# Attention in front of a mixture of experts: the row of maxima carried by a second copy of the queries, and a batch's work in another order

## What is computed

```python
scores = jnp.einsum('bkgsd,bktd->bkgst', qh, kh) / scale     # qh: normalised x, scale = 4
weights = jax.nn.softmax(scores, axis=-1)
out = jnp.einsum('bkgst,bktd->bkgsd', weights, vh)
...
x = x + jnp.tanh(g_xattn[0]) * _L0_xattn_ref(_layernorm(x, axis=-1), ctx_512, ctx_512)
x = x + jnp.tanh(g_ffn[0]) * _L0_ffn_ref(_layernorm(x, axis=-1), ...)
```

## Time and profile before

| | us |
|---|---|
| median of 3 runs | 1440.05 |
| lowest, highest | 1434.08, 1441.21 |
| the profiled execution | 1444.12 |
| its span | 1442.2 |
| PE busy in the span | 1332.6 (92%) |
| DVE busy | 932.8 (65%) |
| ACT busy | 543.3 (38%) |
| POOL busy | 412.3 (29%) |

### The profile page before, as it was taken

How to read it: one execution, slowest core, us unless ns; L and a number is a source line. 1 busy time by engine, 2 the same in 40 slices (tenths; PEclk the granted TensorE clock), 3 DMA queues, 4 the chain that set the end, 5 groups by cost and what they waited for, 6 DMA issues and landing times.

```text
span 1442.2 us, 33176 instructions
## 1 busy us (share of the span) xinstructions
PE 1332.6 (92%) x12082; PEld 918.3 (64%) x12082; DVE 932.8 (65%) x1627; ACT 543.3 (38%) x847; POOL 412.3 (29%) x470
## 2 busy tenths in 40 slices
PE   3799989797895789989999999999999999999996
PEld 2444444444442667777777777777777777777773
DVE  4897787979765896855545555545444444446887
ACT  2666666767655432222222222222222222222220
POOL 4565455545443710011111111111111111004454
PEclk9965575859555589999999999999999999999998
DMA  6443333334332751136255363546163631167665
GB/s 241 140 133 113 110 132 131 132 104 137 110 133 99 267 190 60 59 132 205 73 179 191 124 212 102 194 144 222 60 211 124 197 108 59 44 212 234 212 206 188
DMA packets 98794, 213.50 MB, mean 148 GB/s; under 512 B 11824, under 2 KB 12336, under 8 KB 98736
## 3 DMA queue, kind: packets, MB, share of 16 engines
q1 hardware_dynamic: 87536, 176.02, 36.1%
q0 software_dynamic: 11200, 36.71, 8.1%
HBM read 228.26 MB, written 66.06 MB: 204 GB/s over the span
## 4 chain that ended last, share of the span: by engine, by line
PE 82%; DVE 8%; issue 4%; DMA 3%; ACT 2%; POOL 1%; DVEq 0%; SPq 0%; ACTq 0%; POOLq 0%
PE PS L1395 38%; PE PS L1414 19%; PE PS L1268 5%; PE PS L1240 5%; PE PS L1252 3%; PE PS L1383 3%; PE PS L1276 3%; DVE negm L841 2%; PE PS L1222 2%; PE PS L1256 1%; DVE xn L827 1%; DMA xnd<-xhl 1%; DMA negR<-negT 1%; PE PS L1286 1%; DVE st L798 1%
## 5 line engine op out<-in xcount | busy, mean ns | idle before, releaser
L1414 PE MATMUL PS<-wb,ghl 128*128 128x512 f16 x1296 | 291.5, 382 | 5.8 <-issue 3.2
L1395 PE MATMUL PS<-uhl,wb 128*128 128x256 f16 x2592 | 293.5, 273 | 2.1 <-DVE uhl L1090 2.1
L1395 PE MATMUL PS<-xT,wb 128*128 128x256 f16 x2592 | 291.8, 273 | 1.1 <-DVE xT L1080 1.1
L1395 PEld LDWEIGHTS PS<-xT,wb 128*128 128x128 f16 x2592 | 253.5, 98 | 30.6 <-issue 1.2
L1395 PEld LDWEIGHTS PS<-uhl,wb 128*128 128x128 f16 x2592 | 252.2, 98 | 31.5 <-DVE uhl L1090 2.4
L1414 PEld LDWEIGHTS PS<-wb,ghl 128*128 128x128 f16 x1296 | 127.4, 98 | 149.9 <-issue 10.2
L841 DVE TENSOR_REDUCE negm<-PS 128x8 f16<-128x1024 f32 x128 | 156.1, 1220 | 75.2 <-PE PS L1240 65.5
L604 POOL COPY ixr<-idx 128x2 int32 x38 | 7.0, 184 | 604.0 <-PE PS L1383 478.4
L1097 DVE TENSOR_TENSOR g<-sl,u 128x512 f32<-128x512 f32 x108 | 74.7, 691 | 146.9 <-ACT sl L761 146.8
L761 ACT ACTIVATE sl<-PS,bb 128x256 f32<-128x256 f32 x216 | 90.5, 470 | 209.7 <-PE PS L1395 209.7
L752 ACT ACTIVATE u<-PS,bb 128x256 f32<-128x256 f32 x216 | 90.4, 470 | 197.0 <-PE PS L1395 164.0
(11 more groups left out here) (153 smaller groups left out, 1597.3 us busy)
## 6 DMA issues: line engine op xcount, KB each, us to landing
wb<-wsc SPq DMA_DIRECT2D x126, 1024.0 KB
wst<-in_wall SPq DMA_DIRECT2D x32, 768.0 KB, 5.9
wsc<-whl SPq DMA_DIRECT2D x32, 768.0 KB, 4.2
ysl<-yb SPq DMA_DIRECT2D x46, 512.0 KB
bd<-in_bdown SPq DMA_DIRECT2D x42, 256.0 KB
X<-in_x SPq DMA_DIRECT2D x8, 1024.0 KB, 8.5
xnd<-xhl SPq DMA_DIRECT2D x32, 256.0 KB, 3.0
xs<-xnd SPq DMA_DIRECT2D x32, 256.0 KB
```

Source lines behind the costliest of these rows:

```text
L1395: ins = pe.matmul(bank[:, hf, (m % 2) * TT:(m % 2 + 1) * TT], wb[:, par, l, k, w, m * P:(m + 1) * P], rhs(x, k), start=(n == 0), stop=(n = ...
L1414: ins = pe.matmul(PS[2][:, t, :], ghl[:, x, k, t * P:(t + 1) * P], wb[:, par, 2, k, w, :], start=(n == 0), stop=(n == len(TERMS) - 1))
```

## The change

The one-row pass is dropped. `negR` becomes `qB`, of the same size: a second copy of a batch's transposed queries, made by a DMA from `qT` (`queries_again`, 256 KB). The row of maxima is then written by DMA over row 16 of each strip of `qB`, and row 16 of the second key version holds ones (a memset on POOL at the start) where it held zeros. So the second pass, now of 32 rows, multiplies the low keys by the high queries and subtracts the maxima in one product. The other 15 rows of low queries meet zeros. SP waits for the copy before it sends a batch's first row of maxima.

The lists of PE, DVE, ACT and SP are put in a new order. The core of the diff, with lines left out:

```diff
+            def queries_again(half, par, quad):
+                b = number(half, par)
+                if isinstance(b, int) and b < 2:
+                    sp.wait_ge(S["qT_ready"], b + 1)
+                else:
+                    sp.wait_ge(S["t_done"], UNITS * (b - 1))
+                sp.dma_start(qB[:, par, :, :, :], qT[:, quad, :, :, :]).then_inc(qB_in[par], 16)
             def neg_rows(half, par, pair):
+                if pair == 0:
+                    sp.wait_ge(qB_in[par], 16 * (half + 1))
+                    sp.nop(nofuse=True)
                 sp.wait_ge(S["negT_ready"], 2 * number(half, par) + pair + 1)
-                sp.dma_start(negR[0::STRIP, par, pair, :, :], negT[:, pair, :]).then_inc(neg_in[pair], 16)
+                sp.dma_start(qB[D::STRIP, par, pair, :, :], negT[:, pair, :]).then_inc(neg_in[pair], 16)
...
                 if nx is not None:
                     neg_rows(*nx[:2], 1)
+                if after is not None:
+                    queries_again(*after)
...
+            for par in range(2):
+                g.memset(kx[:, par, 1, :, 1, 0:1], 1.0).then_inc(S["vone"], 1)
...
                 exps(half, par, 1)
+                if not start:
+                    evac_o(*((half - 1, 1) if par == 0 else (half, 0)), 1)
                 if after is not None:
                     evac_q(*after)
-                if not start:
-                    evac_o(*((half - 1, 1) if par == 0 else (half, 0)), 1)
                 exps(half, par, 2)
+                evac_o(half, par, 0)
+                exps(half, par, 3)
                 weights_hi(half, par)
-                exps(half, par, 3)
-                evac_o(half, par, 0)
...
-                for w, rows in ((0, STRIP), (1, D)):
+                for w in range(2):
                     for odd in range(2):
-                        part = strip(u, odd, rows)
-                        pe.matmul(Tb[:, odd, :], kT[part, quad, w, u // 2, :], qT[part, quad, u // 2, :, :].rearrange("p m c -> p (m c)"),
-                                  start=w == 0, stop=False)
-                for odd in range(2):
-                    part = strip(u, odd, 1)
-                    ins = pe.matmul(Tb[:, odd, :], one16[part, :], negR[part, par, u // 2, :, :].rearrange("p m c -> p (m c)"),
-                                    start=False, stop=True)
+                        part = strip(u, odd, STRIP)
+                        moving = (qT[part, quad, u // 2, :, :], qB[part, par, u // 2, :, :])[w]
+                        ins = pe.matmul(Tb[:, odd, :], kT[part, quad, w, u // 2, :], moving.rearrange("p m c -> p (m c)"),
+                                        start=w == 0, stop=w == 1)
                 ins.then_inc(S["t_done"], 1)
+                if ahead is not None:
+                    scores_max(*ahead)
```

More of the change, by code:

```diff
@@ L192, in program @@
         neg_in = [sem(f"neg_in{j}") for j in range(2)]
+        qB_in = [sem(f"qB_in{j}") for j in range(2)]
         x_in = [sem(f"x_in{c}") for c in range(XC)]
@@ L324, in body @@
                 nx = follow(half, par, quad, 1)
+                after = follow(half, par, quad, 2)
                 start = isinstance(half, int) and number(half, par) == 0
@@ L893, in body @@
                 start = isinstance(half, int) and number(half, par) == 0
[L894 to L898, removed]
+                fourth = follow(half, par, quad, 4)
                 if nx is not None:
                     maxes(*nx[:2], 1)
+                if after is not None:
+                    evac_k(*after)
+                if nx is not None:
+                    maxes(*nx[:2], 2)
                 if not start:
                     normalise(*pv, 0)
-                if after is not None:
-                    evac_k(*after)
                 if isinstance(half, int) and number(half, par) + 2 < XC:
@@ L907, in body @@
                 if nx is not None:
-                    maxes(*nx[:2], 2)
-                weights64(half, par)
+                    evac_neg(*nx[:2], 0)
+                if not (isinstance(half, int) and number(half, par) < 2):
+                    stats2(half - 1, par)
                 if nx is not None:
                     maxes(*nx[:2], 3)
-                    evac_neg(*nx[:2], 0)
-                if not start:
-                    normalise(*pv, 1)
+                if isinstance(half, int):
+                    v.wait_ge(S["ln1_ready"], chunks_by(number(half, par) + 1))
+                if fourth is not None:
+                    norm1(*fourth[:2])
+                weights64(half, par)
                 if isinstance(half, int) and number(half, par) == 1:
@@ L918, in body @@
                     maxes(*after[:2], 0)
-                if not (isinstance(half, int) and number(half, par) < 2):
-                    stats2(half - 1, par)
+                if not start:
+                    normalise(*pv, 1)
                 if nx is not None:
@@ L1228, in strip, with max_waits @@
                 return slice(STRIP * s, STRIP * s + rows)
[L1230 removed]
+            def max_waits(half, par, u):
                 b = number(half, par)
@@ L1301, in body @@
                 pv = (*((half - 1, 1) if par == 0 else (half, 0)), (quad - 1) % 4)
-                scores_T(half, par, quad, 0)
-                if nx is not None:
-                    scores_max(*nx, 1)
-                if not start:
-                    tr_o(*pv[:2], 0)
+                scores(half, par, quad, 0, nx and (*nx, 1))
                 if after is not None:
                     tr_k(*after[:2])
-                scores_T(half, par, quad, 1)
-                if nx is not None:
-                    scores_max(*nx, 2)
+                if not start:
+                    outputs(*pv, 1)
+                scores(half, par, quad, 1, nx and (*nx, 2))
                 if after is not None:
```

43 lines of the change are left out of this document (24 added, 19 removed).

## The result

| | before | changed |
|---|---|---|
| median, us | 1440.63 (4 runs) | 1375.84 (4 runs) |
| lowest, highest | 1434.08, 1442.82 | 1374.13, 1377.42 |
| profiled execution's span | 1442.2 | 1372.2 |

The ratio of the changed kernel to the one before is 0.9557, with a 95% interval of 0.9524 to 0.9591; a second comparison, on the chip of e5, e6 and e7, gave 0.9546 (0.9505 to 0.9586).

The account below looks back on a forecast made before the run. PE bounds a batch at clock 0.50, DVE at 1.00. 23 batches saving 1.35 us each (31), plus 3 for the last three, less 1 at the start, gave 33 off 1440.05: 1407 us, range 1378 to 1431.

Parts of the forecast that it names:

- the share of full clock: Attention batches: 32% of the time at full clock, from a mean clock of 0.66, kept for the new kernel.
- The forecast's 11.5: Attention from batch 6 on: a batch takes 11.5 us against 12.85, saving 1.35 each in 23 batches, 31 us.
- a clock far from 0.66: Sign of being wrong: mean clock between 129 and 400 us, moving the result by up to 20 us either way.
- The rival with the higher clock: Attention: two thirds of the time at full clock, batch 10.6 us, about 55 us saved, 1385 us; chance 0.16.
- The rival with the low clock: Attention: PE's idle time and three transposes in a row keep clock 0.50, batch 12.1 us, 1426 us; chance 0.17.
- PE's unit: PE's score unit at clock 0.50: 0.97 us without the one-row pass, against 1.39, four times a batch.
- DVE's queries: DVE's normalised queries, behind the third maxima: 0.54 us instead of 2.32 beside POOL, upper bound 1.2 more.
- DVE's sum: DVE's instructions per batch: 9.3 us against 11.1; with waits and gaps, a batch of 10.0 us at full clock.
- The first six batches: Start of the attention, with DVE's input statistics of about 2.8 us: no gain, plus or minus 5 us.
- The last batches and the end: Last three attention batches: about 1 us saved each, 3 us.
- The copy of the queries: DMA of 256 KB per batch: 2 us taken, 5.9 the upper bound, no wait expected for the row of maxima.
- the walk's 12.1 us: One batch followed across engines at clock 0.50: DVE, not PE, closes the loop, 12.1 us against 13.46.

Follow-up runs that it names:

- e5: Changed kernel plus a dead pass of one row per strip before each unit's scores: 1376.83 us, 0.9549 of the kernel before.
- e6: Changed kernel plus a dead pass of 32 rows per strip before each unit's scores: 1364.71 us, 0.9481 of the kernel before.
- e7: Changed kernel with DVE's normalised queries moved behind the copy of the keys: 1404.64 us, 0.9746 of the kernel before.
- e9: Changed kernel with three passes and separate row of maxima restored, second pass over 32 rows instead of 16: 1377.38 us, 0.9537 of the kernel before.
- e10: Kernel before with only its second pass widened from 16 to 32 rows: 0.9915 of the kernel before, 1430.27 us.
- e3: Changed kernel with DVE's normalised queries back at the head of its list: 1375.88 us, 0.9492 of the kernel before.
- e14: Kernel before with only DVE's second normalisation moved behind the fourth maxima and the statistics: 1397.78 us, 0.9689 of the kernel before.
- e1: Kernel before with two passes, `qB`, its copy and the row of ones, every engine's list as it was: 1434.37 us, 0.9895 of the kernel before.
- e4: Changed kernel with DVE's statistics moved ahead of the second maxima: 1359.15 us, 0.9365 of the kernel before.
- e2: Changed kernel with `negR` and three passes restored, leaving only the reordered engine lists: 1411.16 us, 0.9735 of the kernel before.
- e11: Changed kernel with the maxima's second product over 32 rows per strip instead of 16: 1364.26 us, 0.9450 of the kernel before.
- e13: Changed kernel with DVE's statistics ahead of the second maxima and a dead pass of 32 rows: 1343.65 us, 0.9321 of the kernel before.

## Why the prediction was wrong

**The step that failed is the clock.** The sum held the share of full clock at 32%, with the words that nothing in the rows says why it is what it is. It became about 74%. By the changed kernel's own batches, 9.29 us at 1.00 and 11.40 at 0.70, a clock of 0.66 would go with some 11.7 us, if the line is drawn on that far. The forecast's 11.5 was for that clock. What came is 10.29, so by that line the clock is worth about 1.4 us in each of 23 batches, 32 us. By the prediction's own two batches, 12.1 and 10.0, a share of 74% gives 10.48 instead of 11.35, 20 us in all. Of the 70 us of span 37 were missing in the forecast, so the clock is 20 to 32 of them. The rest is in the batch at full clock, shorter than forecast, and in the first and the last batches (below). The prediction named a clock far from 0.66 as a sign of being wrong, worth up to 20 us.

**The rival with the higher clock was nearer, for half of its reason.** At two thirds of full clock it gave 1385, and its argument was that the dropped pass used one row, so what is left is denser. e5 and e6 show that rows count and that the drop doesn't: a dead pass of one row leaves clock and time as they are, one of 32 rows takes the clock to 1.00. What the fold changed is that the low keys' pass has 32 rows where it had 16, and e9 gets the whole effect by that alone. The prediction wrote that "rows cost nothing is what the three passes show", which is true of a pass's duration, and stopped there.

**The rival with the low clock fell.** The Trainium skill (TensorE: Matmul & The Clock Gate, Part 1) says that activity releases the throttle. In the prediction the trace of before spoke against it, since its fully busy batch was the slow one. Busy time as the profile counts it is still no measure for it: e6's PE is busy 173.16 of 190 us at clock 1.00, and that of the kernel before 174.62 at 0.63. What raised the clock here was more rows in the same products (e6, e9, e10); whether that is what the page means, no run shows. Three transposes in a row, which the rival feared, stand in batches at clock 1.00, as in the one from 228.24.

**PE's unit was right:** 0.97 forecast, 0.98 measured. But it was costed as a gain of 0.42 us four times in a batch, and it is worth next to nothing: e5 pays a pass back and loses nothing measurable. At full clock the pass is 0.2 us, and PE has that room.

**DVE's queries were right in size and wrong in reason.** 0.53 us was measured where 0.54 was forecast, and as far as the reason goes that was luck. It was put down to their new place behind the third maxima. e3 has them back at the old place and is as fast; what matters is the second normalisation, which releases POOL, and which moved behind the fourth maxima. The prediction used that order in dating POOL and didn't see that it was the edit. Its worth was hidden inside DVE's sum; alone it is 3.1% (e14), three times what the fold with its wider rows brings in the old order (e1, 1.05%).

**DVE's sum was too large.** 9.3 us plus 0.7 of waits gave 10.0 at full clock, and 9.29 was measured, with DVE busy 8.43. The durations of rows overlap: the queries' 0.53 at 228.24 and the scaling of weights behind them at 228.69 share 0.08 us. At a dozen rows per batch that is the difference. The old sum, 11.1, was too large by as much. A batch of the kernel before at full clock, between two starts of the queries:

```profile
249.24:259.70 10.46, 8.21 (x130) 4.31 (x124) 10.20 (x15) 8.58 (x11) 5.56 (x6) 1.00 0.37 122
```

The stretch of 12.40 us in the earlier trace rows is longer than a batch and has the queries of the next one in it, at 3.01 us. So the gain at full clock was forecast nearly right, 1.1 against 1.2. The waits forecast are there: 0.54 us of PE for the fourth maxima (0.6 forecast) and 0.70 of DVE (0.45 forecast).

**The rest held.** The first six batches gained 3.4 us in all (0, plus or minus 5, forecast): they take 13.7 us each, and e4 shows that the statistics on the loop are why. The last batches and the end gained 7.5 where 3 were forecast. The copy of the queries landed after 2.4 us (2 taken; the row is of the page of the changed kernel), and no unit waited for a row of maxima in the later batches:

```profile
qB<-qT SPq DMA_DIRECT2D x32, 256.0 KB, 2.4
```

A full batch at 0.50 doesn't occur in the changed kernel, so the walk's 12.1 us stays untested.

**What stays open.** Why moving one normalisation raised the clock to 0.85 (e14), while the whole new order, which also has it behind the fourth maxima, reached 0.73 (e2); why e11 stops at 0.91 while e6 and e13 reach 1.00; and why e1's clock is 0.79 though PE stands still for 2.3 us in a batch. The runs show that rows bear on the clock, and that the order of the lists does, not by what rule.

## What to carry to other kernels

Before costing a pass by its columns, look at which clock the stage runs and at what moves it: here 16 more rows of zeros in one pass were worth all that the fold brought in the new order, and a dead pass made the kernel faster by under 1%. When an instruction's duration varies fourfold, find its neighbour and what releases that neighbour; the cheapest edit may be on the releaser, as with one normalisation moved by two places for 3.1%. And take apart a change of several edits by undoing each: the dropped pass, for which this one was made, brought nothing measurable in the new order.

## What was not expected of the hardware

- Two kernels with the same products and columns, and a dead pass over 1 or 32 rows per strip, ran at a mean granted clock of 0.88 and 1.00 (130 to 320 us of one execution each), with medians of 1376.83 and 1364.71 us.
- Widening a pass from 16 to 32 rows whose added keys are zero raised the clock from 0.73 to 0.88 in the new order and from 0.63 to 0.81 in the old one. The added rows' zero products don't prevent it.
- DVE's 128x512 instruction between two tiles took 0.53 us alone and 2.0 to 3.3 us where it began inside POOL's 3.10 us instruction. Where the order freed it (e14), DVE's scaling of weights met POOL instead, and took up to 1.8 us, median 1.4, for 0.95.
- A copy of 256 KB between two tiles on the chip landed in 2.4 us (median of 32, 2.3 to 4.3).
